# Blocks of 256 rows in place of 384 in a routed feed-forward kernel, with part of VectorE's work on ScalarE and GpSimd

## What is computed

```python
# x: (32, 256, 256) = 8192 rows of 256; 8 experts, 2 per row; hidden width 1024
scale = 1.0 / np.sqrt(256); ys = cond * scale
d = rsqrt(einsum('bi,io->bo', ys * ys, w * w) + 1e-8)
z = einsum('bsi,io->bso', x * ys[:, None, :], w) * d[:, None, :]
logits = z @ Wr + br
route_w = softmax(logits); keep the two largest, renormalize -> routed
h = relu(einsum('bsd,edh->ebsh', z, W1) + b1)
expert_out = einsum('ebsh,ehd->ebsd', h, W2) + b2
out = x + einsum('bse,ebsd->bsd', routed, expert_out)
```

## Time and profile before

| | us |
|---|---|
| median of 3 runs | 952.39 (951.58 to 953.37) |
| profiled execution, its own time | 952.91 |
| its span in the profile | 951.1 |
| granted TensorE clock over the span | 0.977 of full speed |

### The profile page before, as it was taken

How to read it: one execution, slowest core, us unless ns; L and a number is a source line. 1 busy time by engine, 2 the same in 40 slices (tenths; PEclk the granted TensorE clock), 3 DMA queues, 4 the chain that set the end, 5 groups by cost and what they waited for, 6 DMA issues and landing times.

```text
span 951.1 us, 20960 instructions
## 1 busy us (share of the span) xinstructions
PE 894.1 (94%) x6510; PEld 884.2 (93%) x6510; DVE 752.1 (79%) x1438; ACT 580.8 (61%) x1019; POOL 541.6 (57%) x453
## 2 busy tenths in 40 slices
PE   5982999999999999999999999999999999999993
PEld 4972889999999999999999999999999999999993
DVE  3777679889888778878888878888888788788783
ACT  5856566678876656556556556556565565565561
POOL 6873344535445246666656657657656656566572
PEclk9996899999999999999999999999999999999997
DMA  7895575944354354423444334234334234244232
GB/s 247 286 334 192 183 219 117 270 107 103 80 133 86 72 141 84 88 52 83 89 95 84 50 89 89 48 86 89 55 80 92 51 84 88 51 100 78 45 45 22
DMA packets 52072, 104.26 MB, mean 110 GB/s; under 512 B 7104, under 2 KB 34272, under 8 KB 51264
## 3 DMA queue, kind: packets, MB, share of 16 engines
q0 software_dynamic: 27360, 38.36, 24.4%
q1 hardware_dynamic: 20544, 61.09, 19.5%
q10 hardware_dynamic: 4128, 4.33, 1.4%
HBM read 75.78 MB, written 36.35 MB: 118 GB/s over the span
## 4 chain that ended last, share of the span: by engine, by line
PE 81%; DMA 5%; DVE 4%; issue 3%; ACT 2%; POOL 2%; ACTq 1%; SPq 0%; DVEq 0%; POOLq 0%
PE psum L1447 13%; PE psum L1460 13%; PE psum L1462 12%; PE psum L1461 12%; PE psum L1449 12%; PE psum L1448 12%; PE psum L1426 2%; DMA out<-in_x 2%; DMA x_buf<-in_xT 1%; PE psum L1344 1%; PE psum L1345 1%; POOL out L591 1%; PE psum L1346 1%; DMA raw<-in_experts 1%; DMA z_row<-z_rows,idx_early 1%
## 5 line engine op out<-in xcount | busy, mean ns | idle before, releaser
L790 ACT ACTIVATE h<-psum,b_all 128x384 f32<-128x384 f32 x376 | 218.1, 580 | 278.4 <-PE psum L1449 238.9
L1460 PE MATMUL psum<-w_hi,h_hi 128*128 128x256 f32 x1128 | 318.4, 282 | 2.4 <-DVE h_lo L1282 2.1
L1462 PE MATMUL psum<-w_hi,h_lo 128*128 128x256 f32 x1128 | 318.3, 282 | 0.0
L1461 PE MATMUL psum<-w_lo,h_hi 128*128 128x256 f32 x1128 | 317.9, 282 | 0.0
L1447 PE MATMUL psum<-z_hi,w_hi 128*128 128x384 f32 x752 | 258.5, 344 | 3.1 <-DVE z_lo L1239 2.1
L1233 DVE TENSOR_TENSOR w_lo<-raw,w_hi 128x1024 fp32r<-128x1024 f32 x190 | 232.4, 1223 | 27.9 <-ACT w_hi L727 25.8
L1448 PE MATMUL psum<-z_lo,w_hi 128*128 128x384 f32 x752 | 254.0, 338 | 0.0
L1449 PE MATMUL psum<-z_hi,w_lo 128*128 128x384 f32 x752 | 253.9, 338 | 0.0
L591 POOL DMA_INDIRECT out<-y,idx_put x102 | 225.3, 2209 | 49.1 <-POOL idx_put L587 26.7
L1282 DVE TENSOR_TENSOR h_lo<-h,h_hi 128x384 fp32r<-128x384 f32 x376 | 209.9, 558 | 22.8 <-ACT h L790 11.0
L1460 PEld LDWEIGHTS psum<-w_hi,h_hi 128*128 128x128 f32 x1128 | 212.9, 189 | 4.3 <-DVE h_lo L1282 3.7
(11 more groups left out here) (201 smaller groups left out, 827.3 us busy)
## 6 DMA issues: line engine op xcount, KB each, us to landing
raw<-in_experts SPq DMA_DIRECT2D x64, 512.0 KB
x_buf<-in_xT SPq DMA_DIRECT2D x16, 512.0 KB, 7.5
d_rep<-d_rows SPq DMA_DIRECT2D x4, 1056.0 KB, 7.6
z_rows<-z_all ACTq DMA_DIRECT2D x2, 2112.0 KB, 14.7
z_rows<-z_all SPq DMA_DIRECT2D x1, 2112.0 KB, 13.3
z_rows<-z_once SPq DMA_DIRECT2D x1, 2112.0 KB, 11.1
out<-y,idx_put POOLq DMA_INDIRECT x102
z_row<-z_rows,idx_get POOLq DMA_INDIRECT x99
```

What stands on the lines that cost most here:

```text
L790: act.activation(h[c % NHP][:], h_ps[c % HP][:, 0:TB], ACT.Relu, bias=b1_all[:, ds(e, 1), c]).then_inc(s_relu, 1)
L1460: pe.matmul(yp, hi, w2(w_hi, c), start=(c == 0), stop=False)
L1461: pe.matmul(yp, hi, w2(w_lo, c), start=False, stop=False)
L1462: ins = pe.matmul(yp, lo, w2(w_hi, c), start=False, stop=(c == HC - 1))
```

## The change

Blocks have two tiles of 128 rows: `Q` = 2, TB = 256, so the unrolled blocks number 25 (`N1` = ceil((8192 - 8 x 255) / 256)). `h` gets a third PSUM bank, the one that the third tile of y leaves. The rounding of h for chunks 3, 6 and 7 is on ScalarE in every block, loop included. The low part of weight quarter 1 (`POOL_LO`) is computed by GpSimd, in its queue between the gather and the wait for y, with a semaphore of its own; VectorE computes the other three. The pieces of the second half's routing are spread over the 25 blocks, at most three per block on VectorE.

```diff
-    Q = (out.shape[0] - T) // P
+    Q = 2
-    HP = 2
+    HP = 3
+    POOL_LO = 1
-        h_ps = [bank[i] for i in range(HP)]
+        h_ps = [bank[0], bank[1], bank[NHP + Q + DC]]
-        def back(c):
+        def back(c, n):
-            return NHP if c >= NHP else c + 1 + (HC - 1 - c) % NHP
+            return n if c >= n else c + 1 + (HC - 1 - c) % n
+        def nth_lo(k):
+            return k - (k > POOL_LO)
         def act_hi(b, c):
-            return isinstance(b, int) and b < N1 - 1 and c in ACT_HI
+            return c in ACT_HI
...
                 for k in range(NQ):
                     sp.wait_ge(s_raw[k], g * 16)
-                    sp.wait_ge(s_wlo, b * NQ + k + 1)
+                    if k == POOL_LO:
+                        sp.wait_ge(s_wlo_pool, b + 1)
+                    else:
+                        sp.wait_ge(s_wlo, b * (NQ - 1) + nth_lo(k) + 1)
                     load_weights(g % E, k)
...
+            def weights_lo(b, k):
+                pool.wait_ge(s_whi, b * NQ + k + 1)
+                pool.tensor_tensor(out=w_lo[k][:], in0=raw[k][:], in1=w_hi[k][:].bitcast(f32),
+                                   op=ALU.subtract).then_inc(s_wlo_pool, 1)
...
                     fetch(b + 1, idx_all, z_rows)
+                weights_lo(b, POOL_LO)
                 if b == 1:
                     pool.wait_ge(s_init, INIT * 16)
...
             with pool.Fori(N1, n) as b:
                 row_free(b)
                 gather(b + 1)
+                weights_lo(b, POOL_LO)
                 y_ready(b - 1)
                 scatter_add(b - 1)
...
-            TURN = {2: (1, 2), 6: (3, 4), 7: (5,)}
+            TURN = {2: (1,), 6: (2,), 7: (3,)}
...
-                    if c == 5:
-                        weights_lo(b + 1, 1)
                     if is_early(b):
                         for t in TURN.get(c, ()):
-                            second_half(b * 5 + t)
+                            second_half(b * 3 + t)
...
-            weights_lo(0, 1)
...
             def first_product(b, c, fresh):
-                if c % CQ == 0:
-                    pe.wait_ge(s_wlo, (b + 1) * NQ + c // CQ + 1)
+                if c % CQ == 0 and c // CQ == POOL_LO:
+                    pe.wait_ge(s_wlo_pool, b + 2)
+                elif c % CQ == 0:
+                    pe.wait_ge(s_wlo, (b + 1) * (NQ - 1) + nth_lo(c // CQ) + 1)
                 if not (fresh and c < HP):
-                    pe.wait_ge(s_relu, b * HC + c + 1 - HP)
+                    pe.wait_ge(s_relu, b * HC + c + 1 - back(c, HP))
```

More of the change, by code:

```diff
@@ L327, in bass_adaln_moe_ffn @@
         s_wlo = sem("s_wlo")
+        s_wlo_pool = sem("s_wlo_pool")
         s_idxg = sem("s_idxg")
@@ L736, in second_half @@
             def second_half(b, c):
-                if (b, c) == (0, 7):
+                if (b, c) == (1, 1):
                     act.wait_ge(s_latepick, 3)
                     act.activation(expo[:], logit[:], ACT.Exp).then_inc(s_exp, 1)
-                if (b, c) == (3, 6):
+                if (b, c) == (5, 7):
                     act.wait_ge(s_latepick, N_PICK)
@@ L745, in second_half @@
                                       z_of_group[g]).then_inc(s_zst[g], 16)
-                if (b, c) == (5, 6):
+                if (b, c) == (8, 7):
                     act.wait_ge(s_negrow, 2)
                     aways(2, 1, LATE_ACT[0], 0)
-                if (b, c) == (5, 7):
+                if (b, c) == (9, 1):
                     aways(2, 1, LATE_ACT[0], 1)
-                if b == 6 and c in (0, 2):
-                    hot_scaled(1, c // 2)
-                if (b, c) == (6, 3):
+                if b == 9 and c in (4, 6):
+                    hot_scaled(1, (c - 4) // 2)
+                if (b, c) == (10, 3):
                     row_hot_of(2)
-                if (b, c) == (6, 6):
+                if (b, c) == (11, 1):
                     aways(3, 1, LATE_ACT[1], 0)
-                if (b, c) == (6, 7):
+                if (b, c) == (11, 5):
                     aways(3, 1, LATE_ACT[1], 1)
-                if (b, c) == (7, 3):
+                if (b, c) == (12, 3):
                     row_hot_of(3)
-                if (b, c) == (7, 6):
+                if (b, c) == (12, 6):
                     aways(4, 1, LATE_ACT[2], 0)
-                if (b, c) == (7, 7):
+                if (b, c) == (13, 1):
                     aways(4, 1, LATE_ACT[2], 1)
-                if (b, c) == (8, 3):
+                if (b, c) == (13, 5):
                     row_hot_of(4)
-                if b in (8, 9) and c in (0, 2):
-                    g = HG + (b - 8) * BG + c
+                if b in (13, 15) and c in (0, 2):
+                    g = HG + (b - 13) // 2 * BG + c
                     partial_of(g)
                     partial_of(g + 1)
-                if b == 8 and c in (6, 7):
-                    col_of_of(1, 0, c - 6)
-                if (b, c) == (9, 3):
+                if b == 14 and c in (0, 1):
+                    col_of_of(1, 0, c)
+                if (b, c) == (15, 3):
                     for a in range(2):
@@ L784, in block_of_act @@
                     if not (fresh and c < NHP):
-                        act.wait_ge(s_hlo, b * HC + c + 1 - back(c))
+                        act.wait_ge(s_hlo, b * HC + c + 1 - back(c, NHP))
                     if act_hi(b, c):
@@ L1050, in early_tables @@
                 for k in range(NQ):
-                    dve.memset(began[:, k:k + 1], 0.0).then_inc(s_wlo, 1)
+                    dve.memset(began[:, k:k + 1], 0.0).then_inc(s_wlo_pool if k == POOL_LO else s_wlo, 1)
                 last(s_block)
@@ L1265, in block_of_dve @@
             def block_of_dve(b, fresh):
-                given = sum(act_hi(b - 1, c) for c in (HC - 2, HC - 1)) if isinstance(b, int) and b >= 1 else 0
+                given = 0 if fresh else 2
                 if not fresh:
@@ L1404, in second_half @@
             def second_half(b, c):
-                if (b, c) == (3, 1):
+                if (b, c) == (5, 1):
                     ranks(1)
-                if (b, c) == (7, 6):
+                if (b, c) == (12, 6):
                     pe.wait_ge(s_hot2, 2 * TOPK)
@@ L1411, in second_half @@
                         parts(1, g)
-                if (b, c) == (8, 6):
+                if (b, c) == (14, 2):
                     for g in range(HG + BG, NTG):
                         parts(1, g)
-                if (b, c) == (9, 6):
+                if (b, c) == (16, 2):
                     pe.wait_ge(s_psb, NTG)
                     columns(1)
-                if (b, c) == (11, 2):
+                if (b, c) == (18, 6):
                     table(1)
```

## The result

The changed kernel takes 1201.18 us (1196.56 to 1204.72, four runs) beside 952.88 us (951.58 to 953.87) for the kernel before on the same chip: a ratio of 1.2597, with the interval 1.2555 to 1.264. The forecast was 1018 us. The direction is right, the size is not: the time is 106 us above the end of the range.

The account below looks back on a forecast made before the run. TensorE bounds the old kernel; with 256 rows its 11.8 us a block becomes 12.5 through late helpers and GpSimd's product. 98.7 + 68 x 12.5 + 24.7 + 15.7 + 7.9 + 20 = 1017 us of span, forecast 1018, range 990 to 1045.

Parts of the forecast that it names:

- the end of the run: Last block and its scatters: 31.7 us before, less a shorter block and one scatter, leaves 24.7 us.
- 15.7: Time lost in the first 14 blocks of the kernel before, over 17.5 us a block; carried over unchanged.
- the 20 us: First 25 blocks: `second_half` work between h_lo6 and h_lo7 in some 18; bad order in half, 9 x 2.2.
- The wait in front of the weights: At the start, block 2's low weights queue on GpSimd behind its wait for copies of x: 7.9 us, once.
- late helpers: Per block, TensorE loses 0.2 us before S2, 0.1 before S5, 0.2 before S7: 12.3 us, not 11.8.
- the product's end: GpSimd's product, falling on z_lo and y, holds up r_cur and the first cast 0.1 to 0.3: 12.5 a block.
- VectorE is first in a steady block, by 0.3 us: Block's end: h_lo7 starts at 11.1, GpSimd's product is ready at 11.4, so it falls on z_lo and y.
- Rival 3: Port lost every block: GpSimd precedes h_lo7, S7 waits 2.2 us more, 14.7 a block, 1148 us; chance 0.10.
- Rival 1: TensorE still sets the pace, the helpers' latenesses vanish: 11.8 us a block, 943 us; chance 0.13.
- Rival 2: Helpers late, port harmless: 12.3 us a block, without the 20 us, 984 us; chance 0.22.
- Rival 4: ScalarE's four register loads at each block's start delay relu 0 some 1.5 us: 13.5 a block, 1066 us; chance 0.12.
- The third bank: Extra PSUM bank for h: costs nothing, lets F3 wait for relu 0, cover two banks would also have had.

Follow-up runs that it names:

- Experiment 1: Changed kernel plus one wait: GpSimd's low weight product starts only after VectorE's last `h_lo` of the block before; 1018.8 us, 1.0705.
- experiment 2: Changed kernel with the low part of weight quarter 1 back on VectorE, behind `h_lo` of chunk 5; 1037.82 us, 1.0905.
- experiment 7: Changed kernel with 20 unused 256-column matmuls on TensorE ahead of S7 in every loop block; 1183.82 us, 1.2451.
- experiment 4: Kernel before, blocks of 384 rows, with ScalarE's roundings in every block and GpSimd's low weight product, unordered; 1014.23 us, 1.0657.
- experiment 8: Changed kernel's 256-row blocks alone: two banks for h, all low parts and the loop's roundings on VectorE; 1057.49 us, 1.1113.
- experiment 12: Changed kernel with GpSimd's product cut to 512 of 1024 columns, unordered, the other half left out; 1096.14 us, 1.1512.
- experiment 3: Changed kernel with GpSimd's product cut into four pieces of 256 columns, no new wait; 1044.74 us, 1.0995.

## Why the forecast was wrong

**What was right.** Almost all of the sum. Experiment 1 is the kernel in the order that the forecast laid out, and it takes 1018.8 us for the 1018 said. Term by term, measured there: the first mark at 95.6 us for 98.7; steady blocks of 12.61 for 12.5; the end of the run 24.2 (1016.8 - 992.6) for 24.7, where the forecast's own terms, 31.7 - 5.5 - 1.8, give 24.4. Everything above the steady block in the first 24 intervals is 341.2 - 24 x 12.61 = 38.6 us, where the forecast had 15.7 + 7.9 + 20 = 43.6: the sum agrees partly by luck, as the 20 us were for a held `h_lo` that this run doesn't have, while two other terms were too small. The wait in front of the weights is 9.3 us (49.9 less the 40.6 of experiment 2's first three intervals) for 7.9. The other 29.3 us stand where the forecast took over 15.7 from the blocks of 384 rows; what they consist of isn't taken apart. The 0.7 us a steady block over TensorE's 11.8 (0.5 for late helpers, 0.2 for the product's end) is there in sum, 0.8, but not all where it was put. The chain through one block of experiment 1 shows three long steps where a matmul of 256 columns takes 0.12 (start, length):

```profile
803.79 0.35 PE psum L1463
...
806.88 0.36 PE psum L1463
...
813.71 0.39 PE psum L1476
```

The last is S7, which does wait for `h_lo`. The second is F4, behind the low part of the third quarter. The first is F2, which starts within 0.2 us of the end of GpSimd's product (801.22 + 2.40 = 803.62). S2 and S5 hardly wait.

**The step that failed** is the one that let the product on GpSimd fall on z_lo and y: "VectorE is first in a steady block, by 0.3 us". In the changed kernel the two start within 0.15 us of each other by the record (807.00 and 807.07, 821.90 and 822.05), and VectorE, though its record starts first, is the one that waits, in 60 of 69 blocks. GpSimd has no gap there: its gather's record ends at 807.05 and the product's starts at 807.07. The forecast's margin of 0.3 us came from a layout in which `h_lo` of chunk 7 starts 3.8 us behind the copy `r_next` and the product 4.1 us behind it. Measured are 4.0 and 4.15 us in the 15 us blocks, 4.25 and 4.32 in the 16 us ones: a margin of 0.06 to 0.17 us, and by the record it wasn't enough. Everything past it costs 2.3 us; the forecast gave that case 1 in 10. It should have had the chance of a coin's toss at least. The order doesn't need a hold in the block before to come about: in one block of the loop the product stands 4.95 us behind `r_next` and `h_lo` takes 0.42 us (at 716.32), and the next block's `h_lo` is held again, 2.70 us. The two meet because both hang on `r_next` at nearly the same distance. In the first 25 blocks the forecast counted the bad order nine times; it came in 18.

**Rival 3 is what happened**, with its mechanism and nearly its price: 2.2 us more for S7 was said, 2.3 measured. It gave 1148 us and fell 53 short of the median, 49 short of the profiled execution (1196.56). Of these, 36 lie in the last 44 intervals, 15.51 us each for 14.7, and 16 in the first 24, 392.6 us for 24 x 14.7 + 15.7 + 7.9 = 376.4; the first mark gives 3 back. TensorE's clock is one part, which no rival had: in about every other block half speed follows the wait and costs 1 us, 0.4 us a block on average and 17 us in all by experiment 7. Without it a stretch from one `h_lo` of chunk 7 to the next is experiment 1's 12.62 us and the hold: 14.99 with 2.37 held, 15.06 with 2.44 held in experiment 7. What lengthens the first 24 intervals isn't taken apart; nor is why the clock falls behind some waits of 2.4 to 2.5 us and not behind others.

**The port rule.** Cited was the Trainium skill's "SBUF — State Buffer", section "Who interferes with whom": an instruction of VectorE with two inputs in SBUF and one of GpSimd that reads SBUF exclude each other for the whole instruction. Most of it the runs bear out: `h_lo` is held by the product (2.71 us for 0.42), for the rest of that instruction's length (1.74 with half of it, 1.70 for 0.56 in experiment 4, where the product began 1.1 us earlier), not by a memset that only writes (0.42), and z_lo and y, with an input in PSUM, not at all. "Whoever starts first" can't be read from the record where the two start together: by its starts VectorE was first with the whole, the half and the quarter product alike, and it waited for the first two and not for the third. The forecast read the earlier trace rows for this and saw the small side of it, because GpSimd's instructions before were descriptors and copies; of the two sides it used the one in which VectorE wins.

**The other rivals.** Rival 1 (TensorE alone sets the pace, 11.8 us a block) is refuted: even with the port out of the way a block is 12.61. Rival 2 (12.3, port harmless, 984) is close to experiment 1's loop but not to its total. Rival 4 (register loads) came only once: the loads take 0.28 us each by the median in the changed kernel and at most 0.29 in its loop, as in the case in which they are hidden; in one block near 190 us the four take 0.95 to 1.76. The third bank, put down as free cover, is worth 0.09 us a block.

**The parts of the 249 us.** By differences of whole runs: the size alone +106 (experiment 8); the roundings on ScalarE and the third bank -20 (8 to 2); GpSimd's low part, ordered, -19 (2 to 1); the order that was left to chance +182 (1 to the changed kernel). At 384 rows the two moves without the size cost 9 us ordered and 63 us unordered.

## What to carry to other kernels

Before work moves to GpSimd, list which VectorE instructions with two SBUF inputs stand near it, and order it behind the one on the critical path by a wait (pieces help too, with less certainty); a layout that is good by a few tenths of a microsecond is no protection where the miss costs the whole instruction. A smaller block saves only what padding it takes away, while every cost per block, weights above all, is paid more often: here 384 padded rows less bought 22 more conversions of a whole set of weights. When TensorE's idle time comes in one piece per block, look at the granted clock too: the wait may cost more than its length.

## What the runs showed of the hardware

- The engine whose record starts first isn't always the one that goes first: `h_lo` at 807.00 waited for a product on record from 807.07, at 821.90 for one from 822.05, and in experiment 12 at 805.61 for one from 805.78, but in experiment 3 at 811.33 it went ahead of a piece from 811.50. Once, in the changed kernel, an `h_lo` on record from 1008.89 was held 3.33 us although the product is on record only from 1009.59, 0.69 us later, when an `h_lo` alone would have ended. So GpSimd's recorded starts can't be trusted to a few tenths of a microsecond; why the short piece lost is open.
- A copy of two columns into `r_cur` is caught too: 0.17 us alone, 0.38 beside the product's end in experiment 1, and 0.67 (from 719.03) in the one block of the changed kernel's loop in which the product comes late.
- An idle time of 2.4 to 2.5 us in a block of 15 was followed by half speed in 23 of 43 blocks, for 12 to 15 matmuls, and cost 1 us each time: granted clock 0.94 over the steady part, 1.00 when the idle time was filled with matmuls of no use.
- The product on GpSimd costs 2.36 us for 1024 columns, 1.27 for 512, and 0.73 for 256: about 0.2 us an instruction and 2.1 ns a column.
